# Three streamed cross attentions: the two top scores of a unit move behind its score groups in TensorE's order

## The reference

```
q = split_heads(x @ Wq + bq);  k = split_heads(context @ Wk + bk);  v = split_heads(context @ Wv + bv)
scores  = einsum('bhqd,bhkd->bhqk', q, k) * hd ** -0.5
weights = softmax(scores, axis=-1)
out     = einsum('bhqk,bhkd->bhqd', weights, v)  ->  out @ Wo + bo
```

## Time and profile before

| | us |
|---|---|
| median of three runs | 3316.8 |
| profiled execution, whole | 3317.55 |
| its span | 3315.8 |
| TensorE matmul busy | 2940.3 (89%) |
| VectorE busy | 1830.3 (55%) |
| ScalarE busy | 1350.1 (41%) |
| GpSimd busy | 402.9 (12%) |

### The profile page before, as it was taken

One profiled execution on the slowest core, in us unless ns is written; L12 is line 12 of the kernel. 1 busy time (PEld: TensorE's weight loads), 2 busy tenths in 40 slices (PEclk: granted clock), 3 DMA queues, 4 the chain that ended last, 5 costly groups with the idle time before them and its releaser, 6 DMA issues. The chain is left out here.

```text
span 3315.8 us, 66524 instructions
## 1 busy us (share of the span) xinstructions
PE 2940.3 (89%) x27158; PEld 2482.7 (75%) x27158; DVE 1830.3 (55%) x3246; ACT 1350.1 (41%) x2191; POOL 402.9 (12%) x571
## 2 busy tenths in 40 slices
PE   7999669995959997659998769999999999999978
PEld 6998537773827775636776646999999999999867
DVE  5556357774247773548774434555555555555424
ACT  4555226672106664215665111444443444444311
POOL 2444300001000000000000004020202020100000
PEclk9999869997959997879998766999999999999969
DMA  5888688851868880369882351110101010000016
GB/s 157 301 322 332 264 174 176 177 120 51 283 131 169 175 177 26 122 166 180 176 176 55 136 164 39 40 40 1 40 1 40 1 40 1 1 1 1 17 52 230
DMA packets 204581, 393.95 MB, mean 119 GB/s; under 512 B 33491, under 2 KB 164948, under 8 KB 201588
## 3 DMA queue, kind: packets, MB, share of 16 engines
q1 hardware_dynamic: 202599, 388.90, 43.9%
q10 hardware_dynamic: 1680, 0.80, 0.1%
HBM read 289.45 MB, written 99.49 MB: 117 GB/s over the span
## 5 line engine op out<-in xcount | busy, mean ns | idle before, releaser
L729 DVE TENSOR_REDUCE L_xattn_tops<-psum 128x1 f32<-128x896 f32 x672 | 702.4, 1086 | 272.4 <-PE psum L591 271.1
L652 ACT ACTIVATE L_xattn_probs<-psum 128x512 f32<-128x512 f32 x1176 | 612.1, 601 | 483.1 <-PE psum L602 483.1
L1737 DVE TENSOR_TENSOR L_units_low<-psum,L_units_high 128x896 fp32r<-128x896 f32 x224 | 243.6, 1087 | 486.1 <-ACT L_units_high L1686 486.1
L591 PE MATMUL psum<-L_xattn_keys,L_xattn_q_stack 96*128 96x448 bf16 (+1 forms) x1344 | 394.8, 378 | 113.0 <-DMA L_xattn_q_stack<-query_parts 66.0
L1654 PE MATMUL psum<-wide_tokens,L_units_high 128*128 128x386 f32 x1568 | 455.8, 359 | 1.4 <-DVE L_units_low L1737 1.4
L602 PEld LDWEIGHTS psum<-L_xattn_q_stack,L_xattn_keys 99*128 99x128 bf16 (+1 forms) x4704 | 322.3, 98 | 143.9 <-issue 18.6
L602 PE MATMUL psum<-L_xattn_q_stack,L_xattn_keys 99*128 99x128 bf16 (+1 forms) x4704 | 393.3, 221 | 5.0 <-ACT L_xattn_probs L652 5.0
L1655 PE MATMUL psum<-wide_tokens,L_units_low 128*128 128x194 f32 x1568 | 394.5, 252 | 0.0
L615 PE MATMUL psum<-L_xattn_probs,L_xattn_values 128*17 128x128 f32 x9408 | 357.0, 276 | 0.4 <-ACT L_xattn_probs L652 0.2
L1686 ACT CAST L_units_high<-psum 128x896 fp32r<-128x896 f32 x224 | 203.1, 907 | 363.5 <-PE psum L1642 363.5
L1678 ACT ACTIVATE L_units_raw<-L_units_raw,L_units_negmax 128x896 f32<-128x896 f32 x224 | 221.5, 1036 | 307.6 <-DVE L_units_negmax L1728 307.6
(11 more groups left out here) (436 smaller groups left out, 3985.9 us busy)
## 6 DMA issues: line engine op xcount, KB each, us to landing
key_parts<-proj_parts SPq DMA_DIRECT2D x84, 672.0 KB, 4.2
L_xattn_keys<-key_parts SPq DMA_DIRECT2D x144, 336.0 KB, 4.7
values_scratch<-proj_values SPq DMA_DIRECT2D x21, 1904.0 KB, 7.9
L_xattn_values<-values_scratch SPq DMA_DIRECT2D x144, 238.0 KB, 5.2
L_ffn_w<-in_L_ffn_W SPq DMA_DIRECT2D x32, 1024.0 KB, 6.8
L_xattn_keys<-key_parts SPq DMA_DIRECT2D x144, 224.0 KB, 5.0
L_xattn_keys<-key_parts SPq DMA_DIRECT2D x192, 112.0 KB, 5.0
L_ffn_w<-in_L_ffn_w SPq DMA_DIRECT2D x16, 1024.0 KB, 6.9
```

The source lines that it names most:

```text
L591: last = pe.matmul(top_slot(n)[:, s, :], q_stack[0:P1, h, :], keys[0:P1, v % RING, key:key + WIN // 2], start=True, stop=True)
L652: act.activation(group_probs(k), score_bank(k), ACT.Exp).then_inc(sem("probs"), 1)
L729: dve.tensor_reduce(tops[:, h % 2, 2 * c + w:2 * c + w + 1], top_slot(n), AX.XY, ALU.max)\
L1737: dve.tensor_tensor(low[gr][:], turned_banks(gr), high[gr][:], ALU.subtract).then_inc(sem("low"), 1)
```

## The change

In the loop over u, the first half's top scores move from the front of a unit to behind its second score group, and the second half's from behind the second group to behind the third.

```diff
                     ahead, now = v < NU, 0 <= u < NU
-                    if ahead:
-                        top(v, 0)
                     if now:
                         scores(k)
                         scores(k + 1)
                     if ahead:
-                        top(v, 1)
+                        top(v, 0)
                     if now:
                         scores(k + 2)
-                        if u % 2 == 0:
-                            scores(k + 3)
+                    if ahead:
+                        top(v, 1)
+                    if now and u % 2 == 0:
+                        scores(k + 3)
```

## The result

The changed kernel takes 3309.95 us as the median of 15 runs, against 3316.8 for the kernel before (15 runs beside them). The ratio is 0.998, with a 95% interval of 0.9973 to 0.9987. That is 6.8 us faster. I had forecast 3301, a gain of 16.

The account below looks back on a forecast made before the run. TensorE was taken to set the pace in the three stages, at 2.7 us a unit. A gain of 17 us less 0.6 at stage starts, about -16.4, gave 3301 us, range 3288 to 3315.

Parts of the forecast that it names:

- The stall removed: Even units: TensorE's 0.11 us wait for the exponential three groups back goes, in 149 units; gain taken as 17 us.
- Sums behind a top: Odd units: sums now follow top scores; entry taken as 0.09 us, as behind a score group, so no cost.
- the dear entry: Rival, odd units: entering the sums behind a top costs 0.21 us, +18 us, ending at 3317 to 3319; chance 0.11.
- the hidden entry: Rival, odd units: entering the sums behind a top costs nothing, 14 us more gained, 3287; chance 0.09.
- Sums ahead of scores: After the sums, scores follow instead of a top; still 0.99 us as in the tail, so no cost.
- VectorE's slack: VectorE's reductions: the next second top still finds its slot free, slack 0.35 us (0.55 before), cost 0.
- A head's maximum: Transposed maxima, copied before a head's first scores: margin falls from 1.53 to 0.59 us, cost 0.
- The rival of a late maximum: Maximum arrives after a head's first scores, stopping TensorE in the first unit of 45 heads: 3337 us; chance 0.07.
- The stage start: Start of each stage: scores now stand in front and wait for the copies; 0.2 us a stage, 0.6 in all.
- the moved stall: Rival, even units: exponentials stay late in the ring of three banks, no gain, 3316 to 3318; chance 0.09.

Follow-up runs that it names:

- the short exponentials: Kernel before, with exponentials of all but a stage's first 14 groups over 384 of 512 columns: 3300.2 us, ratio 0.9949.
- the early transpose: VectorE's transpose of the maxima put ahead of its unit's second reduction: 0.9959 on the changed kernel, 0.9997 on the kernel before.
- the change again: The changed kernel rerun with no edit, against the kernel before: 3310.16 us, ratio 0.9983.
- the change with the early transpose, again: Rerun of the changed kernel with VectorE's transpose of the maxima ahead of its unit's second reduction: 3296.66 us, ratio 0.9943 to the kernel before.
- late-transpose: Changed kernel with VectorE's transpose of the maxima put off behind the next unit's first reduction: 3388.68 us, ratio 1.0217 to the kernel before.

## Why the prediction was wrong

**The stall removed** was right in place, size and cause. Even units went from 2.85 to 2.74, where 2.74 was written. The count of 149 holds, and the short exponentials show the cause.

**Sums behind a top** were right: odd units 2.52 as written, 0.48 from the last top to the sums for 0.47, so neither the dear nor the hidden entry came. The order in even units alone and the new order everywhere, both with the early transpose, agree with it. **Sums ahead of scores** and **VectorE's slack** were right too: in the three windows inside the stages the waits after the change have no top that waits for VectorE.

**A head's maximum** is the step that failed: "a margin of 1.53; left are 1.53 - 0.44 - 0.39 - 0.11 = 0.59. Cost 0." The arithmetic of the shifts was right, but it was done at the wrong consumer. I took the head's first scores to be those of its first unit and read the margin at one head, the even one of the earlier trace rows. At that very head the margin after the change is 0.58, from these rows, as forecast; at the other 20 even heads it went from about 1.83 to 0.87 or 0.89, so the row read was not even typical of its own parity.

```profile
579.64 1.01 POOL L697 COPY L_xattn_q_stack<-L_xattn_max_rows 4x32 bf16<-4x32 bf16 x4 [4.46 <-DVE L_xattn_max_rows L740]
...
581.23 0.62 PE L602 MATMUL psum<-L_xattn_q_stack,L_xattn_keys 100*128 100x128 bf16 x8
```

For the other parity the consumer is the fourth group of the unit before, 98 tiles not being a multiple of four. There the margin was 0.08 (copies' end at 559.25, the group at 559.39, less 0.06 from the copies' end to the release), and the stall that the change takes away, 0.11 to 0.12, made all of it. Without the stall the copies are some 0.04 late even where nothing delays them, as the new order in even units alone shows. Lateness 0.44 against 0.08 of margin, with the group 0.11 earlier, gives 0.47; 0.49 was measured, in 21 units, 10.3 us. The rival of a late maximum had the mechanism but the wrong place, "the first unit of 45 heads", and the wrong threshold, so it got 0.07 and a price of 36 us that never came. At the low size that it took, it ends on the faster side.

**The stage start** was sized at 0.2 us a stage. From the first top to the first sums the three stages took 27.66, 27.66 and 27.47 us for 26.83, 27.57 and 27.54 before. The granted clock was at 0.50 over all of these but the 26.83, where it was 0.52, because it rose before the first sums. Between the stretches that were at the low level throughout, 27.66 and 27.57, the order costs 0.09 us. The rest of the first stage's 0.83 is the moment of the rise, and this moment changes from run to run with TensorE's order the same: the first stage took 27.53 us at 0.50 in the change again and 25.79 at 0.54 in the change with the early transpose, again.

Where the early transpose takes the failed term away, the forecast's gain of 16.4 is what the streams give, 16.2 and 15.5 us, and the medians of the two sets, 3304.25 and 3296.66, lie on either side of 3301. That the changed kernel's 3309.95 lies between 3288 and 3315 all the same is luck: the upper part of that range stood for the dear entry and the moved stall, and neither came.

## What to carry to other kernels

Where groups and heads (or any two loops) do not divide evenly, find the first instruction that needs each late result from its semaphore wait and check every parity, not one instance in the timeline. A stall that goes may have been the cover of a second wait right behind it: for each wait at the same instruction, write down its own arrival time, and let the move's shift pass through both. When two producers feed one engine's order, a move of cheap work (one 0.2 us transpose, 1.0 us earlier) can be worth more than the change itself: it took 10.7 us off the streams where the change alone took 5.5. By itself, without the change, it was worth nothing (0.9997).

## What the runs showed of the hardware

In the late-transpose trace a wait of 1.84 us of TensorE, up to 567.64, was followed by a granted clock of 0.50, 1.2 GHz, from 568.60 to 571.90, although the engine was at work again by then. Fourteen of 21 such waits had a slow unit behind them and seven had none; the waits of 0.33 us in the change had no such effect, with the clock at 1.00 in all three windows. This made the late transpose some 21 us dearer than its waits.

Score matmuls of 128 columns, each with weights of its own, keep 0.055 us from start to start. A switch into the sums costs 0.09 to 0.10 behind a score group or behind a top, and one out of them 0.21 ahead of a top or ahead of a score group; these are the pairs that the traces have.
